# First score pass in the first layer's feed-forward stages: two pairs of tiles at a visit, and visits further apart

## The chip, the cores and the metric

The kernel runs on one core of one Trainium2 chip. TensorE (PE) multiplies matrices, ScalarE (ACT) and VectorE (DVE) work on what it leaves in PSUM, GpSimd (POOL) and SyncE (SP) do small work and issue transfers. The metric is the time of one execution on the device, in microseconds (us). Before the change it is 2257.18 us, the median of 3 runs (2246.01 to 2261.7).

## The reference

Four transformer layers with conditioning work on x of shape (4, 512, 288): 4 batch entries, 512 tokens, 288 channels, 16 heads of 18 channels. Each layer computes six modulation vectors from the conditioning input, then an attention block and a feed-forward block:

```
mod = silu(c) @ w_adaln + b_adaln            # shift, scale, gate, twice
h = ln(x) * (1 + scale) + shift
q, k, v = split(h @ w_qkv + b_qkv)
attn = softmax(q @ k^T * 18**-0.5)           # per head, 512 x 512
x = x + gate * (attn @ v @ w_proj + b_proj)
x = x + gate2 * ffn(ln(x) * (1 + scale2) + shift2)
```

In the first layer the feed-forward block is a mixture of 4 experts, each 288 -> 1152 -> 288. A gate picks the top 2 for each token, but all four are computed for all tokens and weighted. The other layers have one such network. In the third layer the attention is of another kind (each token's 16 heads attend to one another; it has its own steps, with "2" or "b" in their names), and the gelu is the exact one.

## The kernel before, in words

**Steps.** `plan` writes one list of steps, and each of the five engine programs walks this list and issues its own part of every step, with semaphores between them. So the list's order is the order on every engine's queue. What is put next is decided by a planned time, `pe[0]`, which adds up the entries of `PE_NS` (ns of TensorE, 1650 for an `fc1`, 400 for an `fc2`, 230 for an `s1`).

**Stages.** A stage of the main loop has number i, 0 to 16. It holds the attention of image i (an image is one batch entry in one layer: i // 4 is the layer, i % 4 the entry), woven with the norm and the q/k projection of image i + 1; then the v projection of image i + 1; then the feed-forward block of image i - 1, woven with two side streams: `mid(i)` (turning the attention output, projection, residual, norm, routing) and `side`, the first score pass of image i + 1.

**Two score passes.** The softmax needs the maximum of each row of scores. The first pass (`s1`) computes a score tile of one head and one block of 128 queries (54 rows of contraction: 18 channels in three blocks of high and low parts; 512 keys wide), and VectorE reduces it to 128 row maxima (`s1_max`, L1496). The two heads of a pair (x = 0, 1) lie on the upper and the lower half of the partitions. An image has 8 pairs x 4 query blocks x 2 heads = 64 such tiles. After four heads (a group g) `rows` transposes the maxima (L1743), and they are stored as further rows of QS (L1111). The second pass (`s2`, L1750) computes the transposed scores with the maxima subtracted, ScalarE exponentiates them (L1345), and `av` (L1760) multiplies with v. The attention has 16 such steps, `st`; step st needs the rows of group st // 4. Each step also takes one turn of the first pass (`s1_step`): of the same image as long as tiles are left, then of the next image, once its q and k have landed.

**The first pass as a stream.** `s1_steps(i)` is a generator. A turn (one `next`) puts one visit: two `s1` tiles, one for each head of the pair, then their two `s1_max`. A `rows` step takes a turn of its own, DEFER = 1 query block into the next pair. Until the transfers of q and k are due (QK_LAND), turns do nothing. `weave(main, sides)` takes the main stream step by step and, at each of its yields, gives a side stream a turn if its gap of planned time has passed since its last one. For the first layer's feed-forward stages the gap of the first pass is `S1_NS[0]` = 5000 (i = 2 to 4, all four experts) and `S1_0_NS[2]` = 4000 (i = 1, experts 1 to 3).

**The feed-forward main stream.** `ffn_steps` works in units of two hidden tiles of 128 x 256 tokens: an `fc1` (14 matmuls, L1856) into bank 6 or 7, ScalarE's two gelus, VectorE's `hid` (the low part of the hidden tile, L1626), and, two units later (LAG), the four `fc2` (3 matmuls each, L1871, and one with the bias, L1869, at the start of a half) into banks 2 and 3. It yields after each `fc1` and after each pair of `fc2`. At the end of a half the gated result is read out (`res`, L1561). In the second half of each expert, weights of the next ones are split into high and low parts by background steps (ScalarE L1375, VectorE L1394 and L1396).

**Banks.** A score tile fills a whole PSUM bank. `ring()` deals banks out in turn: in a first-layer feed-forward stage RING_B = (0, 1, 4, 5), which the middle steps use as well; in the attention RING_A = (0, 1, 7). The second pass uses banks 4 and 5, and 2 and 3. TensorE waits (`may_fill`) until the last reader of the bank is done.

## Time and profile before

| | |
|---|---|
| median of 3 runs | 2257.18 us |
| the profiled execution, its span | 2257.0 us |
| TensorE busy | 2033.0 us, 90% |
| VectorE busy | 1335.6 us, 59% |
| ScalarE busy | 1143.6 us, 51% |
| row maxima (L1496), all 768 | 490.4 us of VectorE, 682 ns each |
| first-pass score tiles (L1737), all 768 | 226.1 us of TensorE |

The span is that of one execution which the hardware profiler recorded. Busy time is the union of an engine's instructions; matmuls overlap in the records, so their durations may not be added up: the distance from one start to the next tells what one costs. In the trace, the first layer's feed-forward blocks lie about at 193 to 428 us (image 0), 497 to 648 (image 1), 710 to 860 (image 2) and 923 to 1069 (image 3), and the attention behind them at 436 to 493 (image 2), 652 to 707 (image 3), 864 to 920 (image 4) and 1070 to 1132 (image 5). The granted clock of TensorE is 1.00 at 2.4 GHz and 0.50 at 1.2 GHz.

### The profile page before, as it was taken

To read this page: it belongs to the slowest core of one execution; us is meant where nothing else is said; L and a number is where in the kernel's file an instruction comes from. 1 tells how busy PE (TensorE), PEld (TensorE's weight loads), DVE (VectorE), ACT (ScalarE), POOL (GpSimd) and SP (SyncE) were. 2 spreads that over 40 slices of the span, in tenths; PEclk is the share of its full clock that TensorE was granted. 3 is DMA by queue.
4 is the path that set the end of the run, shared out by engine and by line. 5 is a ranking of instruction groups with operands and counts; after the bars stand their busy time and mean duration, and the time that the engine had idled before them with its cause. 6 is when DMAs were issued, how large, how long until landed. Compare 5 with 4: busy or idle time off the path is not lost.

```text
span 2257.0 us, 38969 instructions
## 1 busy us (share of the span) xinstructions
PE 2033.0 (90%) x15592; PEld 1509.0 (67%) x15592; DVE 1335.6 (59%) x2940; ACT 1143.6 (51%) x1705; POOL 207.4 (9%) x311
## 2 busy tenths in 40 slices
PE   6978899899989998999799899899888898999898
PEld 4347388658966994788375657788786556464658
DVE  4757637756774767476556673462444849484833
ACT  2444624574655456445626464552443464637373
POOL 2000001202100211012010000011000000000001
PEclk9787989899989999999889999998898998999999
DMA  5333332343333233333322313346254141314011
GB/s 158 77 123 57 100 95 72 79 111 86 89 77 106 72 89 76 96 94 88 94 72 35 103 17 65 73 88 109 34 95 130 7 121 26 99 11 115 9 14 25
DMA packets 204731, 173.97 MB, mean 77 GB/s; under 512 B 54822, under 2 KB 164678, under 8 KB 204550
## 3 DMA queue, kind: packets, MB, share of 16 engines
q1 hardware_dynamic: 197974, 158.76, 30.1%
q0 software_dynamic: 6576, 12.71, 2.1%
q8 instruction: 124, 2.03, 0.4%
q14 instruction: 57, 0.47, 0.1%
HBM read 125.57 MB, written 40.11 MB: 73 GB/s over the span
## 4 chain that ended last, share of the span: by engine, by line
PE 63%; DVE 18%; ACT 12%; DMA 3%; issue 2%; SPq 2%; POOL 0%; ACTq 0%; POOLq 0%; DVEq 0%
PE PSA L1856 16%; PE PSA L1871 13%; DVE MX L1496 7%; PE PSA L1647 5%; PE PSA L1760 5%; PE PSA L1737 5%; ACT PB L1345 4%; PE PSA L1707 4%; PE PSA L1750 4%; PE PSA L1719 2%; DVE FL L1396 2%; PE PSA L1780 1%; ACT FH L1375 1%; PE PSA L1670 1%; DVE HH L1626 1%
## 5 line engine op out<-in xcount | busy, mean ns | idle before, releaser
L1496 DVE TENSOR_REDUCE MX<-PSA 128x1 f32<-128x512 f32 x768 | 490.4, 682 | 296.9 <-PE PSA L1737 293.2
L1856 PE MATMUL PSA<-A,FH 128*128 128x256 f32 x2520 | 445.3, 292 | 12.5 <-DVE HH L1626 9.6
L1871 PE MATMUL PSA<-FH,HH 128*128 128x288 f32 x2016 | 447.7, 313 | 2.0 <-DVE HH L1626 2.0
L1382 ACT ACTIVATE HH<-PSA 128x512 fp32r<-128x512 f32 x252 | 150.4, 597 | 572.5 <-PE PSA L1856 567.3
L1345 ACT ACTIVATE PB<-PSA 128x1024 f32<-128x1024 f32 x384 | 370.9, 1025 | 102.5 <-PE PSA L1750 101.8
L1856 PEld LDWEIGHTS PSA<-A,FH 128*128 128x128 f32 x2520 | 364.9, 195 | 34.6 <-issue 17.3
L1871 PEld LDWEIGHTS PSA<-FH,HH 128*128 128x128 f32 x2016 | 329.7, 195 | 42.3 <-issue 38.0
L1871 PE MATMUL PSA<-FL,HH 128*128 128x288 f32 x1008 | 303.7, 301 | 0.0
L1737 PE MATMUL PSA<-KS,QS 54*128 54x512 f32 x768 | 226.1, 517 | 40.0 <-DVE MX L1496 14.0
L1255 POOL TENSOR_TENSOR X<-X,TM 128x288 f32<-128x288 f32 x128 | 101.1, 808 | 1496.7 <-DVE TM L1561 1496.6
L1760 PE MATMUL PSA<-PB,VT 128*32 128x512 f32 x1536 | 219.6, 637 | 0.0
L1750 PE MATMUL PSA<-QS,KS 56*128 56x512 f32 x768 | 172.6, 498 | 51.2 <-ACT PB L1345 27.2
L1626 DVE TENSOR_TENSOR HH<-PSA,HH 128x512 fp32r<-128x512 f32 x252 | 171.8, 682 | 76.1 <-ACT PSA L1383 75.8
L1856 PE MATMUL PSA<-A,FL 128*128 128x256 f32 x1008 | 208.0, 288 | 6.3 <-DVE FL L1396 6.3
L1871 PEld LDWEIGHTS PSA<-FL,HH 128*128 128x128 f32 x1008 | 196.8, 195 | 0.0
L1750 PEld LDWEIGHTS PSA<-QS,KS 56*128 56x128 f32 x768 | 70.2, 198 | 165.4 <-ACT PB L1345 84.8
L1737 PEld LDWEIGHTS PSA<-KS,QS 54*128 54x128 f32 x768 | 94.3, 203 | 115.1 <-DVE MX L1496 37.8
L1856 PEld LDWEIGHTS PSA<-A,FL 128*128 128x128 f32 x1008 | 159.3, 195 | 10.3 <-DVE FL L1396 9.1
L1383 ACT ACTIVATE PSA<-PSA 128x512 f32<-128x512 f32 x252 | 149.5, 593 | 0.0
L1375 ACT CAST FH<-ST 128x672 fp32r<-128x672 f32 x171 | 123.2, 748 | 32.9 <-PE PSA L1871 13.5
L1396 DVE TENSOR_TENSOR FL<-ST,FH 128x544 fp32r<-128x544 f32 x171 | 125.3, 733 | 5.3
L1707 PE MATMUL PSA<-A,WQ 128*126 128x512 f32 (+1 forms) x300 | 95.5, 421 | 23.0 <-DVE HH L1490 9.5
(166 smaller groups left out, 2261.5 us busy)
## 6 DMA issues: line engine op xcount, KB each, us to landing
qkd<-HH SPq DMA_DIRECT2D x48, 504.0 KB
ST<-in_L_cond_w SPq DMA_DIRECT2D x51, 432.0 KB
ST<-in_L_cond_w SPq DMA_DIRECT2D x102, 192.0 KB
QS<-qkd SPq DMA_DIRECT2D x88, 144.0 KB
KS<-qkd SPq DMA_DIRECT2D x88, 144.0 KB
QS<-qkd SPq DMA_DIRECT2D x144, 72.0 KB
KS<-qkd SPq DMA_DIRECT2D x144, 72.0 KB
ST<-in_L_cond_w SPq DMA_DIRECT2D x153, 48.0 KB
```

The costliest lines, as they stand in the source:

```text
L1345: e.activation(pbf[st % 3][:, p * 1024:(p + 1) * 1024], PSA[:, bk * 512:(bk + 2) * 512], ACT.Exp, scale=SCALE).then_inc(free[bk], 1)
L1382: e.activation(r(HH[u][:, 0, :]), PS[bk][:, :], gelu)
L1383: e.activation(PS[bk][:, :], PS[bk][:, :], gelu).then_inc(s_gelu, 1)
L1396: e.tensor_tensor(r(lo), ST[k % 2][:, s0:s0 + nl], hi[:, 0:nl], ALU.subtract).then_inc(s_wlo, 1)
L1496: e.reduce_max(MX[p // 2 % 2][:, col:col + 1], PS[bk][:, :], axis=AX.X).then_inc(free[bk], 1)
L1626: e.tensor_tensor(r(HH[u][:, 1, :]), PS[bk][:, :], HH[u][:, 0, :], ALU.subtract).then_inc(free[bk], 1)
L1707: m = e.matmul(PS[bk][0:M, :], r(w_), r(x_), start=(z == 0), stop=(z == 6))
L1737: e.matmul(PS[bk][:, :], r(QS[64 * x:64 * x + 54, p, q * 128:(q + 1) * 128]), r(KS[64 * x:64 * x + 54, p, :]), start=True, stop=True).then ...
L1750: m = e.matmul(PS[bk + x][:, :], r(KS[64 * x:64 * x + 56, 2 * g + p, kt * 128:(kt + 1) * 128]), r(QS[64 * x:64 * x + 56, 2 * g + p, :]), s ...
L1760: m = e.matmul(PS[bk][32 * hh:32 * hh + 32, :], VT[:, kt, h * V1:h * V1 + 32], PB[st % 3][:, hh, :], start=(kt == 0), stop=(kt == 3))
L1856: m = e.matmul(PS[bk][:, s_ * 256:(s_ + 1) * 256], r(w_), r(x_[:, half * 256:(half + 1) * 256]), start=(z == 0), stop=(z == 6))
L1871: m = e.matmul(PS[bk][:, 0:C], r(HH[u][:, c, tk]), r(w_), start=False, stop=(j == NCH - 1 and z == 2))
```

## The change

In the feed-forward stages of the first layer (i = 1 to 4) a turn of the first pass puts two query blocks: four `s1` tiles in four banks, then their four maxima, where the block is even; an odd one, left over from a visit of the attention, is done alone first. The gap grows to 8000 ns for all of them. In the attention and in the later layers a visit stays at two tiles. `S1_NS[0]` also stands in the weave behind the feed-forward block.

```
-S1_0_NS = (0, 2500, 4000)
-S1_NS = (5000, 400, 3000)
+S1_0_NS = (0, 2500, 8000)
+S1_NS = (8000, 400, 3000)
...
-    hurry, stream = [False], []
+    hurry, stream, two_visits = [False], [], [False]
...
-            for q in range(QT):
+            q = 0
+            while q < QT:
                 while not hurry[0] and pe[0] < qk_at.get((i, min(g, 2)), 1e9) + QK_LAND:
                     yield
-                bks = []
-                for x in range(2):
-                    bk = ring()
-                    put("s1", i, p, q, x, bk, qk_n[min(g, 2)])
-                    bks.append(bk)
-                for x in range(2):
-                    put("s1_max", p, q, x, bks[x])
+                visit = range(q, q + (2 if two_visits[0] and q % 2 == 0 else 1))
+                q = visit[-1] + 1
+                bks = {}
+                for qq in visit:
+                    for x in range(2):
+                        bk = ring()
+                        put("s1", i, p, qq, x, bk, qk_n[min(g, 2)])
+                        bks[qq, x] = bk
+                for qq, x in bks:
+                    put("s1_max", p, qq, x, bks[qq, x])
                 yield
-                if late is not None and q == DEFER:
+                if late is not None and DEFER in visit:
                     rows(*late)
                     late = None
                     yield
...
+        two_visits[0] = bool(i) and kind == 0
         if i:
             weave(ffn_steps(i - 1, (1, 2, 3) if i == 1 else None), ((m, MID_NS[kind], MID_AT[i == 11] if L == 2 else 0),
                                        (side, S1_0_NS[2] if i == 1 else S1_NS[kind], 0)))
         weave(m, ((side, S1_NS[kind], 0),))
+        two_visits[0] = False
```

## Rows read from the trace of the kernel before

**Rows 1.** The page: span, and busy time of TensorE.

```profile
span 2257.0 us, 38969 instructions
PE 2033.0 (90%) x15592; PEld 1509.0 (67%) x15592; DVE 1335.6 (59%) x2940; ACT 1143.6 (51%) x1705; POOL 207.4 (9%) x311
```

**Rows 2.** Windows: length, busy us of each engine (instructions), granted clock, DMA share.

```profile
497.00:648.00 151.00, 147.05 (x1075) 136.64 (x1073) 101.18 (x207) 77.84 (x130) 22.58 (x34) 0.98 0.30 85
652.00:707.00 55.00, 49.40 (x284) 20.60 (x285) 32.74 (x79) 38.14 (x46) 0.12 (x1) 0.91 0.49 116
```

**Rows 3.** Windows for the maxima alone: PE (transposes), PEld, then DVE.

```profile
497.00:648.00 151.00, 0.55 (x2) 0.18 (x2) 24.45 (x38) 0.98 0.30 85
923.00:1069.00 146.00, 0.54 (x2) 0.18 (x2) 23.25 (x37) 1.00 0.30 78
652.00:707.00 55.00, 0.66 (x2) 0.17 (x2) 15.49 (x25) 0.91 0.49 116
1070.00:1132.00 62.00, 0.56 (x2) 0.18 (x2) 16.93 (x27) 0.89 0.37 100
```

**Rows 4.** Timeline of TensorE, feed-forward: start, duration, line, tiles, count.

```profile
560.68 0.28 PE L1856 MATMUL PSA<-A,FH 98*128 98x256 f32 x1
560.80 0.30 PE L1869 MATMUL PSA<-B,ON 128*128 128x288 f32 x1
...
563.40 0.28 PE L1856 MATMUL PSA<-A,FH 98*128 98x256 f32 x1
563.61 0.49 PE L1737 MATMUL PSA<-KS,QS 54*128 54x512 f32 x2
564.03 0.54 PE L1871 MATMUL PSA<-FH,HH 128*128 128x288 f32 x2
```

**Rows 5.** Timeline of TensorE in image 0's attention: three tiles in a row.

```profile
91.44 0.62 PE L1737 MATMUL PSA<-KS,QS 54*128 54x512 f32 x3
```

**Rows 6.** Timeline of image 2's attention: steps with and without a visit.

```profile
463.30 0.73 PE L1750 MATMUL PSA<-QS,KS 56*128 56x512 f32 x4
463.87 0.39 PE L1737 MATMUL PSA<-KS,QS 54*128 54x512 f32 x2
...
466.24 1.19 PE L1707 MATMUL PSA<-A,WQ 128*126 128x512 f32 x4 [0.98 <-DVE HH L1490]
...
468.04 0.73 PE L1750 MATMUL PSA<-QS,KS 56*128 56x512 f32 x4
...
471.53 0.73 PE L1750 MATMUL PSA<-QS,KS 56*128 56x512 f32 x4
...
464.30 1.29 DVE L1496 TENSOR_REDUCE MX<-PSA 128x1 f32<-128x512 f32 x2 [0.83 <-PE PSA L1737]
465.50 0.68 DVE L1490 TENSOR_TENSOR HH<-PSA,HH 126x512 fp32r<-126x512 f32 x1
```

**Rows 7.** Timeline: hidden tile's low part, and the fc1 two units later.

```profile
501.21 0.69 DVE L1626 TENSOR_TENSOR HH<-PSA,HH 128x512 fp32r<-128x512 f32 x1 [0.30 <-ACT PSA L1383]
502.05 0.36 PE L1856 MATMUL PSA<-A,FH 128*128 128x256 f32 x1 [0.62 <-DVE HH L1626]
...
567.49 0.69 DVE L1626 TENSOR_TENSOR HH<-PSA,HH 128x512 fp32r<-128x512 f32 x1
569.03 0.64 PE L1856 MATMUL PSA<-A,FH 128*128 128x256 f32 x4
...
634.83 0.68 DVE L1626 TENSOR_TENSOR HH<-PSA,HH 128x512 fp32r<-128x512 f32 x1
636.85 0.52 PE L1856 MATMUL PSA<-A,FH 128*128 128x256 f32 x3
```

**Rows 8.** Timeline and a window at the seam to image 3's attention.

```profile
650.84 1.28 DVE L1496 TENSOR_REDUCE MX<-PSA 128x1 f32<-128x512 f32 x2
652.26 1.22 PE L1750 MATMUL PSA<-QS,KS 56*128 56x512 f32 x4 [3.83 <-DVE MX L1496]
...
652.00:661.00 9.00, 7.95 (x29) 2.95 (x33) 7.30 (x20) 5.80 (x7) 0.12 (x1) 0.50 0.88 167
```

## The prediction

> **What bounds the kernel now.** The page first: one profiled execution of 2257.0 us, TensorE busy for 90% of it [rows 1]. Then the windows of the stages that the edit touches. In a feed-forward window of the first layer (497 to 648 us) TensorE is busy for 147.05 of 151 us and VectorE for 101.18; in the attention window behind it (652 to 707 us) TensorE for 49.40 of 55 us [rows 2]. So a feed-forward stage ends with TensorE's own work, and there I may only gain by giving TensorE less to do; an attention stage has idle time to gain. Then the same windows for the row maxima alone, one of which follows each first-pass score tile: 38 and 37 in two feed-forward windows, 25 and 27 in two attention windows, 0.64 us of VectorE each (24.45 / 38) [rows 3]. Last the timelines: what a visit costs TensorE among the feed-forward matmuls [rows 4], what more tiles in a row cost [rows 5], what a visit costs in an attention step [rows 6], how close VectorE's part of the hidden tile comes to the next fc1 [rows 7], and the seam of the two stages [rows 8].
>
> **How many visits there will be.** PE_NS gives the planner's clock. 36 units of one fc1 (1.65) and four fc2 (1.6) are 117 us, the middle steps some 10, the score tiles the rest. The loop yields after an fc1 and after each fc2 pair, so a gap is rounded up to the next yield. Before, a gap of 5 becomes mostly 6.5 (two units) plus the visit's own 0.46: about 21 turns, of which 2 go to the row transposes: 19 visits, 38 tiles, as counted [rows 3]. After, a gap of 8 becomes 8.1 (two and a half units) plus 0.92: about 15 turns, 3 for transposes, 12 double visits: 48 tiles. An image has 64 tiles (8 pairs, 4 row blocks, 2 heads), and the step list has 8 of them in the attention before, behind the landing of its keys. For images 3, 4 and 5 that leaves 64 - 8 - 48 = 8 tiles to their own attention instead of 18. For image 2 (the stage with i = 1, 27 units, old gap 4, rounded to about 4.3 for one visit and now 8.1 for a double one) the counts stay level, 36 or so against 38.
>
> **Term A, TensorE in the feed-forward stages.** From the last fc1 matmul to the first fc2 matmul it is 0.12 us (560.68 to 560.80), with a visit between 0.63 us (563.40 to 564.03): a visit adds 0.52 us (between 0.63 and 0.66 less 0.12) [rows 4]. The two tiles of a pair of heads run side by side; a third tile starts 0.23 us behind them, since three take 0.62 us where two take 0.39 [rows 5, 6]. So a double visit adds 0.52 + 0.23 = 0.75 us, and not 1.04: what is saved is one entry and one exit, 0.29 us. Images 3 to 5: 19 x 0.52 = 9.9 against 12 x 0.75 = 9.0, three times -0.9 = -2.7. Image 2: 9.9 against 9 x 0.75 = 6.8, and one visit more is left to the attention: -3.1. A = -5.8. The other bound: were the 0.29 us a cost of each pair, A would be 3 x (12 x 1.04 - 9.9) + (9 x 1.04 - 9.9) = +7.2. I take -5.8, because the row of three tiles shows the third without it. The Trainium skill (TensorE Tiling (Array Packing), Key Properties) says that a change of the tiling mode drains TensorE; by it the price belongs to the change between 54-row and full-height matmuls, and the sum would be -5.8 rather than +7.2. The trace's third tile agrees.
>
> **Term B, the attention of images 3 to 5.** Two steps of the same make stand side by side: with a visit and a qk tile, 463.30 to 468.04, 4.74 us; with the qk tile alone, 468.04 to 471.53, 3.49 us [rows 6]. The difference, 1.25 us, is mostly a wait of 0.98 us: ring banks 0, 1 and 7 are filled by two score tiles and one qk tile, so each qk tile needs the bank of the one before it, whose subtraction (HH, 465.50) stands behind two maxima (464.30, 1.29 us) on VectorE. Images 3, 4 and 5 each have three such steps, the seventh to the ninth; with 8 tiles left the visits end in the fourth. Two of the three are as in the row: -2.5 us. The first qk step also waits for the turned activations, so it gives 0 to 1.25: I take 0.6. Two steps with a transpose lose a visit worth about 0.25 us: -0.5. Together -3.6 each (bounds -2.5 and -4.5), times three: -10.8. Image 2's one visit more falls on a qk step: +1.2. B = -9.6 (bounds -6.3 and -12.5).
>
> **Term C, what four maxima in a row delay.** They hold VectorE for 2.6 us where two hold it for 1.3. Queued behind them in program order are the hidden tile's low part (L1626), the weight splits and the gated residuals; fc1 two units later waits for the first through its bank, fc1's low terms for the second, fc2 at the start of a half for the third. The slack of that fc1 behind its hidden tile, where a visit stands ahead of it (16 times in the window), was 0.15 us at the first (501.90 to 502.05), 0.85 at 569.03, and 1.34 at the last (635.51 to 636.85) [rows 7]; the 16 lie between 0.15 and 7.0. A double visit delays VectorE by 1.28 more and TensorE itself by 0.23, so slack under 1.05 turns into a stall. Spread over the 16 that is 0.12 us a visit, for twelve visits 1.4. For splits and residuals I add about 1 us a stage, the size of the small waits that these windows have already (4 us idle in 151, [rows 2]). Three stages with 2.4, the shorter one 1.8: C = +9. Bounds: nothing, and twice as much, +18.
>
> **Term D, the seam.** At the end of image 1's feed-forward the last visit's maxima (650.84, 1.28 us) hold a bank that the second score pass needs; TensorE idles for 3.83 us [rows 8]. Four maxima hold it for up to 1.3 us more, if the last visit is again that late; if it comes a gap earlier, 1.3 us are won. Bounds -1.2 and +1.3 in each of three seams; by the yields a visit falls at the end again, so I take +0.5 each: D = +1.5.
>
> Costing nothing: the extra two banks of a visit. Ring B has four, the visit takes all, and the next middle step (at least 0.8 us of fc2 later) needs the first of them, whose maximum has started by then; ScalarE's and the DMA queues' work is neither added nor passed, only the row stores (L1111) come a few us earlier, with their group of heads long before its use. The gap of 8 also holds in the weave that empties the middle steps behind a stage with i = 0, where visits stay single; of these steps none or a few are left by then.
>
> **Sum:** -5.8 - 9.6 + 9 + 1.5 = -4.9, so 2257.0 - 4.9 = 2252 us. The median before, 2257.18, is the profiled time within 0.2 us, so it needs no shift.
>
> **The rivals.**
> 1. *VectorE's backlog wins (slower).* Place: the feed-forward stages, behind each of some 45 double visits. If the 1.05 us is never absorbed, C is 45 x 1.05 = 47 and the time 2257 - 15.4 + 47 + 1.5 = 2290. For it: slacks of 0.15 and 0.85 us, VectorE at 67%, and more where weights are split. Against: slack of over 1.3 us in most units. It decides the sign at C = 14 us (0.3 us a visit), and passes 1% at about 0.8 us a visit.
> 2. *The cover holds.* C and D nothing, A and B as worked out: 2257 - 15.4 = 2242; with the best bounds of B and D, 2235.
> 3. *Attention gives nothing back.* If the qk steps wait for the turned activations or for ScalarE's copies as long as they now wait for HH, B is +1.2 and the time 2257 - 5.8 + 1.2 + 10.5 = 2263. Against: the qk step without a visit, which waited for neither.
> 4. *The clock.* Right behind the idle seam, from 652 to 661 us, the granted clock is 0.50, that is 1.2 GHz, after 3.83 us in which TensorE did nothing [rows 8]. A longer seam could lengthen such a stretch: matmuls there take twice as long, so 3 us more of it in three seams cost some 5 us: 2257. The Trainium skill (TensorE: Matmul & The Clock Gate, Why this matters for your kernels) warns of idle gaps between bursts, which speaks against a late double visit; the trace's seam agrees.
> 5. *The change hardly does what it says*: if visits meet fewer yields than I count and 40 tiles are made, A is near -4, B near -2, C near 7, D as before: 2257 + 2.5 = 2260.
>
> **How the numbers follow.** Forecast as worked out (net gain under 1%): 0.50; the cover holds 0.18; backlog 0.15, about half of it over 1%; no gain in attention 0.08; clock 0.05; few visits 0.04. Range: A + B at their best with C and D at nothing or better reach 2235; C doubled, B's weak end and longer seams reach 2257 - 5.8 - 6.3 + 18 + 3.9 = 2267, with a little clock 2269; A's other bound, +7.2, would carry that to 2280 and is left out, since a row speaks against it. That leaves out most of the backlog's high end and the extreme of the low one: 2236 to 2269. One per cent, about what a measurement of this kernel can tell, is 22.6 us: faster than 2234.6 has 0.07 (the good ends of rival 2), slower than 2279.8 has 0.07 (rival 1), the rest 0.86.
>
> **What would show each step.** A: score visits of four tiles among fc1 and fc2, with about 0.87 us from the matmul before to the one behind. Count: 48 or so maxima in the feed-forward windows of images 1 to 3. B: in images 3 to 5 qk steps of 3.5 us and no wait for HH there; attention windows shorter by 3 to 4 us. C: waits of fc1 for L1626 and L1396, of fc2 for TM, growing from about 2 to about 4 us a stage. D: the idle time before the first second-pass matmul at 3 to 5 us. I am wrong if the waits of C sum to over 15 us, if the attention windows keep their length, or if the seams move by more than 2 us each.

## The result: 1.25% slower, and the profile after

The changed kernel takes 2285.06 us, the median of 4 runs (2279.86 to 2289.14), against 2259.44 us (2246.01 to 2262.4, 4 runs) for the kernel before in the same comparison: a ratio of 1.0125, 95% interval 1.0092 to 1.0159. I had forecast 2252 us, and 2236 to 2269 as the range. The time lies above the range, and the sign is wrong: of the outcomes I named, it is the third, slower by over 1%, to which I had given 0.07.

Line numbers of the kernel after are six higher: L1743 is `s1`, L1502 `s1_max`, L1862 `fc1`, L1877 `fc2`, L1756 `s2`, L1713 `qk`. The page of its profiled execution, span and busy time, answers to [rows 1]:

```profile
span 2283.7 us, 38968 instructions
PE 2043.3 (89%) x15592; PEld 1514.3 (66%) x15592; DVE 1338.2 (59%) x2940; ACT 1143.2 (50%) x1705; POOL 209.0 (9%) x311
```

The span is 26.7 us longer than before. TensorE issues the same 15592 matmuls, yet is busy for 10.3 us more, and idle for 16.4 us more. VectorE and ScalarE have the work that they had. Of the 10.3 us, 7.5 lie ahead of 289.8 us (230.1 us busy before, 237.5 after), where TensorE has the same matmuls in the same order in both and the granted clock is 0.85 before and 0.81 after: that part isn't the change's. What the change costs has to be read from the stages that it touches.

To find the place I cut both traces at the same points: a stage from the start of the v projection of image i to the first second-pass matmul of image i (it holds a feed-forward block and the seam), and the attention from there to the next v projection. First the kernel before, its four stages and four attentions (windows: stretch, length, busy us of PE, PEld, DVE, ACT, POOL with their instructions, granted clock, DMA share, GB/s):

```profile
286.90:436.30 149.40, 140.91 (x952) 126.60 (x950) 86.77 (x177) 60.75 (x103) 21.25 (x32) 0.92 0.30 81
493.10:652.30 159.20, 151.42 (x1106) 140.73 (x1104) 106.07 (x218) 80.18 (x135) 24.12 (x36) 0.98 0.31 88
706.60:863.70 157.10, 149.85 (x1105) 139.34 (x1103) 102.82 (x213) 77.41 (x132) 24.34 (x37) 0.99 0.29 76
919.60:1070.30 150.70, 145.24 (x1077) 134.53 (x1075) 100.00 (x196) 75.17 (x129) 20.22 (x32) 1.00 0.31 82
436.30:493.10 56.80, 48.31 (x280) 19.88 (x280) 34.60 (x91) 39.22 (x48) 7.88 (x11) 0.88 0.36 91
652.30:706.60 54.30, 48.96 (x282) 20.13 (x282) 32.34 (x76) 37.84 (x46) 0.00 (x0) 0.91 0.49 117
863.70:919.60 55.90, 48.74 (x280) 20.12 (x281) 34.61 (x79) 39.03 (x48) 1.87 (x3) 0.91 0.44 108
1070.30:1131.70 61.40, 48.88 (x283) 19.74 (x284) 34.05 (x77) 40.49 (x48) 4.27 (x7) 0.89 0.37 100
```

And the kernel after, the same eight stretches; the last row is a window of the maxima and row transposes alone (PE, PEld, DVE), which answers to [rows 3]:

```profile
289.80:447.30 157.50, 142.16 (x951) 128.17 (x949) 85.61 (x174) 60.71 (x103) 22.60 (x34) 0.90 0.28 77
506.60:678.70 172.10, 156.16 (x1119) 143.92 (x1117) 115.31 (x230) 80.09 (x135) 24.89 (x36) 0.95 0.30 85
729.80:895.10 165.30, 152.09 (x1118) 141.35 (x1116) 110.07 (x226) 77.17 (x132) 26.88 (x39) 0.98 0.27 73
946.50:1103.80 157.30, 148.65 (x1083) 138.00 (x1081) 104.47 (x204) 75.12 (x129) 19.76 (x30) 0.98 0.29 77
447.30:506.60 59.30, 48.65 (x283) 20.08 (x283) 36.55 (x94) 39.22 (x48) 6.27 (x10) 0.89 0.33 82
678.70:729.80 51.10, 47.42 (x265) 18.67 (x266) 24.08 (x62) 37.88 (x46) 0.00 (x0) 0.90 0.48 115
895.10:946.50 51.40, 47.60 (x271) 19.23 (x271) 27.18 (x66) 39.03 (x48) 0.00 (x0) 0.91 0.45 116
1103.80:1158.10 54.30, 45.95 (x276) 18.68 (x275) 30.09 (x69) 40.37 (x48) 5.10 (x8) 0.94 0.41 111
...
506.60:678.70 172.10, 0.82 (x3) 0.27 (x3) 31.78 (x52) 0.95 0.30 85
```

The attentions fell from 228.4 to 216.1 us, by 12.3: the gain came. The four stages grew from 616.4 to 652.2, by 35.8. Length less TensorE's busy time gives its idle time: 29.0 us before, 53.1 after, so 24 us of the 36 are idle time, more than twice the 10.5 that I had allowed in terms C and D. The granted clock fell in each of the four; twice the length times one less the clock is the time at 1.2 GHz, 35 us before and 62 us after where it is summed from the clock's own record. Half of such time is lost, so that is about 13.5 us in this pair of executions. It is firm only in part. In the stages of images 3 to 5 it is 12 us at 1.2 GHz before and 31 after, and runs with the same matmuls in the same order repeat it (10.5 in experiment 8, 28 in experiment 11): a loss of some 10 us. In image 2's stage it is 24 and 31 us; but with that stage's matmuls as before, full maxima and single visits, seven other runs have 11 to 30 us there, and a stage of 144.5 to 152.6 us. So the 3.6 us of the clock there can be chance, and the 8 us by which that stage grew can be off by some us either way. With the visits' -5.8 us (below) and some 4 us that I can't place, this is the whole of it.

### The profile page after: what moved, and what is told of

It reads as the page before. It is cut to its first block, busy times and chain, and to the rows that moved or that the text cites. A ratio compares the mean times of both kernels' runs of the same rounds, so it can differ in the third digit from the quotient of the medians.

```text
span 2283.7 us, 38968 instructions
## 1 busy us (share of the span) xinstructions
PE 2043.3 (89%) x15592; PEld 1514.3 (66%) x15592; DVE 1338.2 (59%) x2940; ACT 1143.2 (50%) x1705; POOL 209.0 (9%) x311
## 4 chain that ended last, share of the span: by engine, by line
PE 63%; DVE 18%; ACT 13%; issue 2%; DMA 2%; SPq 1%; POOL 0%; ACTq 0%; POOLq 0%; DVEq 0%
PE PSA L1862 15%; PE PSA L1877 12%; DVE MX L1502 7%; PE PSA L1766 6%; PE PSA L1653 5%; PE PSA L1743 4%; PE PSA L1756 4%; PE PSA L1713 4%; ACT PB L1351 4%; DVE FL L1402 2%; PE PSA L1676 2%; PE PSA L1725 2%; ACT FH L1381 1%; PE PSA L1786 1%; ACT HH L1388 1%
## 5 line engine op out<-in xcount | busy, mean ns | idle before, releaser
L1502 DVE TENSOR_REDUCE MX<-PSA 128x1 f32<-128x512 f32 x768 | 485.7, 681 | 206.4 <-PE PSA L1743 202.7
L1862 PE MATMUL PSA<-A,FH 128*128 128x256 f32 x2520 | 450.7, 295 | 16.7 <-DVE HH L1632 9.0
L1877 PE MATMUL PSA<-FH,HH 128*128 128x288 f32 x2016 | 442.4, 310 | 2.7 <-DVE HH L1632 2.7
L1862 PEld LDWEIGHTS PSA<-A,FH 128*128 128x128 f32 x2520 | 370.0, 198 | 40.1 <-issue 15.5
L1877 PEld LDWEIGHTS PSA<-FH,HH 128*128 128x128 f32 x2016 | 327.7, 194 | 38.6 <-issue 33.1
L1877 PE MATMUL PSA<-FL,HH 128*128 128x288 f32 x1008 | 301.7, 299 | 0.0
L1743 PE MATMUL PSA<-KS,QS 54*128 54x512 f32 x768 | 222.6, 509 | 53.1 <-DVE A L1478 14.3
L1766 PE MATMUL PSA<-PB,VT 128*32 128x512 f32 x1536 | 224.9, 651 | 0.0
L1862 PE MATMUL PSA<-A,FL 128*128 128x256 f32 x1008 | 211.5, 292 | 15.0 <-DVE FL L1402 14.8
L1756 PE MATMUL PSA<-QS,KS 56*128 56x512 f32 x768 | 174.4, 506 | 53.4 <-ACT PB L1351 29.3
L1632 DVE TENSOR_TENSOR HH<-PSA,HH 128x512 fp32r<-128x512 f32 x252 | 171.5, 681 | 84.9 <-ACT PSA L1389 84.6
L1877 PEld LDWEIGHTS PSA<-FL,HH 128*128 128x128 f32 x1008 | 194.8, 193 | 0.0
L1756 PEld LDWEIGHTS PSA<-QS,KS 56*128 56x128 f32 x768 | 70.9, 201 | 170.5 <-ACT PB L1351 84.7
L1743 PEld LDWEIGHTS PSA<-KS,QS 54*128 54x128 f32 x768 | 94.3, 204 | 129.9 <-DVE MX L1502 37.5
L1862 PEld LDWEIGHTS PSA<-A,FL 128*128 128x128 f32 x1008 | 161.5, 197 | 21.2 <-DVE FL L1402 20.7
L1381 ACT CAST FH<-ST 128x672 fp32r<-128x672 f32 x171 | 122.4, 747 | 26.7 <-PE PSA L1877 14.4
L1713 PE MATMUL PSA<-A,WQ 128*126 128x512 f32 (+1 forms) x300 | 94.9, 418 | 17.3 <-DVE A L1472 10.2
```

The source lines that it names most:

```text
L1502: e.reduce_max(MX[p // 2 % 2][:, col:col + 1], PS[bk][:, :], axis=AX.X).then_inc(free[bk], 1)
L1632: e.tensor_tensor(r(HH[u][:, 1, :]), PS[bk][:, :], HH[u][:, 0, :], ALU.subtract).then_inc(free[bk], 1)
L1713: m = e.matmul(PS[bk][0:M, :], r(w_), r(x_), start=(z == 0), stop=(z == 6))
L1743: e.matmul(PS[bk][:, :], r(QS[64 * x:64 * x + 54, p, q * 128:(q + 1) * 128]), r(KS[64 * x:64 * x + 54, p, :]), start=True, stop=True).then ...
L1756: m = e.matmul(PS[bk + x][:, :], r(KS[64 * x:64 * x + 56, 2 * g + p, kt * 128:(kt + 1) * 128]), r(QS[64 * x:64 * x + 56, 2 * g + p, :]), s ...
L1766: m = e.matmul(PS[bk][32 * hh:32 * hh + 32, :], VT[:, kt, h * V1:h * V1 + 32], PB[st % 3][:, hh, :], start=(kt == 0), stop=(kt == 3))
```

## Where the idle time and the low clock come from

Rows of what TensorE waited for over the four stages and the three attentions between them (engine and line, the releaser, us in total, times, longest), before (287 to 1070 us):

```profile
PE PSA L1856 <- DVE FL L1396: 6.3, 12, 1.8
...
PE PSA L1707 <- DVE HH L1490: 5.7, 7, 1.0
```

and after (289 to 1104 us):

```profile
PE PSA L1862 <- DVE FL L1402: 14.8, 19, 3.7
PE PSA L1756 <- DVE MX L1502: 9.8, 2, 5.0
...
PE PSA L1743 <- DVE A L1487: 5.3, 2, 2.7
PE PSA L1743 <- DVE A L1490: 5.2, 4, 1.3
PE PSA L1743 <- DVE A L1478: 5.1, 4, 1.3
```

Three of these are score tiles (L1743) that wait for the low part of a *turned chunk* of activations (L1478, L1487, L1490). Such a wait hardly existed before. A score tile reads nothing of these chunks: what it shares with them is the ring of banks. Per kernel, over the four stages, TensorE waited 17.4 us ahead of score tiles, 1.2 us before; ahead of `fc1` 23.7 us, 11.2 before; at the seams 9.8 us, 9.5 before.

One of the two longest such waits, at its place in the timeline (start, duration, engine, line, tiles, count, idle time before it with its releaser; weight loads and transfers are left out):

```profile
512.04 0.60 PE L1699 MATMUL PSA<-ID,OT 128*128 128x128 f32 x4
512.28 1.28 ACT L1388 ACT_TABLE_LOAD   x1 [1.33 <-PE PSA L1862]
512.57 0.73 PE L1743 MATMUL PSA<-KS,QS 54*128 54x512 f32 x3
513.57 0.60 ACT L1388 ACTIVATE HH<-PSA 128x512 fp32r<-128x512 f32 x1
514.07 0.59 ACT L1389 ACTIVATE PSA<-PSA 128x512 f32<-128x512 f32 x1
514.58 0.59 ACT L1317 CAST A<-PSA 128x512 fp32r<-128x512 f32 x1
...
515.20 0.69 DVE L1487 TENSOR_TENSOR A<-PSA,A 128x512 fp32r<-128x512 f32 x1 [7.62 <-ACT A L1317]
515.81 2.47 DVE L1502 TENSOR_REDUCE MX<-PSA 128x1 f32<-128x512 f32 x4
515.95 0.79 PE L1743 MATMUL PSA<-KS,QS 54*128 54x512 f32 x1 [2.65 <-DVE A L1487]
```

And the windows right behind it, columns as above:

```profile
516.00:522.00 6.00, 6.00 (x26) 5.56 (x27) 5.47 (x8) 1.78 (x3) 0.00 (x0) 0.50 0.49 134
522.00:531.00 9.00, 7.69 (x56) 6.75 (x56) 4.53 (x9) 4.64 (x8) 0.00 (x0) 1.00 0.65 175
```

At 512.04 four transposes fill a ring bank; the double visit is put right behind them. Three of its tiles start at once, at 512.57. The fourth needs the bank of the transposes, since the visit takes all four. That bank is free only when ScalarE has copied it, behind a table load of 1.28 us and two activations, and VectorE has subtracted. So the fourth tile starts at 515.95, after 2.65 us in which TensorE did nothing, and everything else in its queue stands behind it. In the windows the clock is 0.50, that is 1.2 GHz, for the window of 6 us behind it, in which TensorE is busy throughout, and 1.00 after that. In experiment 11, where this stage has the same matmuls in the same order, the same wait (2.66 us, until 496.70) is followed by a shorter such stretch, 0.50 from 498.0 to 501.4 us and 1.00 from there to 507. In the kernel before the visit behind the same transposes (499.09 us) takes two banks that lie clear of the one just dealt, and waits for nothing. The Trainium skill (TensorE: Matmul & The Clock Gate, Why this matters for your kernels) advises against idle gaps between bursts of matmuls. The trace agrees, with these 2.65 us and the 0.50 behind them, and shows it for a gap shorter than those that the page names.

The `fc1` waits, at one place, same columns:

```profile
817.47 0.73 PE L1743 MATMUL PSA<-KS,QS 54*128 54x512 f32 x4
818.01 2.48 DVE L1502 TENSOR_REDUCE MX<-PSA 128x1 f32<-128x512 f32 x4 [2.05 <-PE PSA L1743]
...
820.84 0.73 DVE L1402 TENSOR_TENSOR FL<-ST,FH 128x544 fp32r<-128x544 f32 x1
...
821.62 0.51 PE L1862 MATMUL PSA<-A,FL 128*128 128x256 f32 x2 [2.65 <-DVE FL L1402]
```

Four maxima hold VectorE until 820.49, a weight's low part follows (to 821.57), and `fc1`'s low terms need it: the delay that the prediction's term C named.

## Experiments

All comparisons are with the kernel before, run on the same chip. "Ring waits" below are TensorE's idle time ahead of score tiles, "fc1 waits" that ahead of `fc1`, "half clock" the time at 1.2 GHz, each summed over the four stages of the profiled execution. That is one execution of each kernel, not its median one; and ahead of image 2's stage, where TensorE's matmuls and their order are the same in all of them, these executions take from 280.6 to 295.9 us. So a few us of half clock, or of a profiled span, tell nothing between two runs.

**1. Many single visits.** The kernel before, with one constant changed, so that about the tiles of the changed kernel move into the stages, two at a visit.

```
-S1_NS = (5000, 400, 3000)
+S1_NS = (4000, 400, 3000)
```

> The kernel before with one number changed: S1_NS[0] from 5000 to 4000, so that single visits (two tiles) come at about the tile rate of the changed kernel (54 tiles in the stages of images 3 to 5, where the changed kernel has 46 to 52 and the one before 38 to 40). Theory R (the bank ring: a double visit fills all four ring banks and waits for a turned chunk): no such wait here, attention of images 3 to 5 shorter by 3 to 7 us each as in the changed kernel, the feed-forward stages longer only by some 7 visits of 0.52 us each, so 2257 - 14 + 11 = 2254 (2246 to 2262). Theory L (it is the higher rate of tiles in the feed-forward stage that delays VectorE and the weight splits, whatever the size of a visit): feed-forward stages 7 to 12 us longer each, 2275 or more.

2267.05 us, ratio 1.0044 (1.002 to 1.0067). It lies between what the two theories said: ring waits 2.5 us and half clock 31 us, as the kernel before has them, but fc1 waits 23.2 us. The tiles themselves also moved (54, 54 and 52 maxima in the stages of images 3 to 5, which take 169.9, 166.9 and 159.9 us). The attention of image 4 reads:

```profile
876.50:928.30 51.80, 48.14 (x267) 19.00 (x267) 24.72 (x62) 38.46 (x47) 0.00 (x0) 0.89 0.47 118
```

It is as short as in the changed kernel (51.40). So moving the tiles costs what it gains and some 10 us more even with single visits (202 maxima in the four stages, where the changed kernel has 188 and the one before 160); the double visits, with image 2's new gap, lose a further 18 us on top.

**2. The gaps alone.** The kernel before with single visits and both gaps at 8000.

```
-S1_0_NS = (0, 2500, 4000)
-S1_NS = (5000, 400, 3000)
+S1_0_NS = (0, 2500, 8000)
+S1_NS = (8000, 400, 3000)
```

> The kernel before with the two gaps of 8000 and single visits: 22 to 28 tiles in the feed-forward stages, 28 to 34 left to the attention. The price of a tile in the attention against one in the feed-forward stage: feed-forward stages shorter by 5 visits of 0.52 us plus what waits they made (3 to 4 us each), attention longer by about 1.3 us for each qk step that gets a visit and 0.3 for the others (3 to 5 us each). Theory R: 2257 to 2265. Theory L: the feed-forward stages gain more than that (5 to 8 us each), 2240 to 2250.

2352.0 us, 1.0436 (1.0393 to 1.0479), slower than either theory said. The stages are shorter, 600.0 us in sum, but the attentions take 91.6, 74.8, 76.9 and 81.8 us. What TensorE waits for in the first of them:

```profile
PE PSA L1750 <- DMA QS<-M: 15.6, 3, 7.5
```

With 28 to 34 tiles left to each attention, the second pass waits for the stores of the row maxima, which both theories had left out. That is a limit to placing fewer tiles in the stages.

**3. Double visits at the old gaps.** The kernel after, with `S1_0_NS[2]` = 4000 and `S1_NS[0]` = 5000.

```
-S1_0_NS = (0, 2500, 8000)
-S1_NS = (8000, 400, 3000)
+S1_0_NS = (0, 2500, 4000)
+S1_NS = (5000, 400, 3000)
```

> The changed kernel with the old gaps (5000 and 4000): double visits only, 56 to 58 tiles in the stages of images 2 to 5, none left to their attention. Theory R: about as many or more visits meet a turned chunk (11 turned or projected banks a stage), so the feed-forward stages lose what the changed kernel loses and a little more, attention gains 2 to 4 us more each: 2278 to 2292. Theory B (four maxima in a row delay the hidden tile's low part and the splits): more visits, more delay: 2290 to 2305.

2269.85 us, 1.0067 (1.0035 to 1.0098), less than either theory said. Ring waits 7.4 us, half clock 46 us, fc1 waits 20.6 us; the seam's idle time is nearly gone (0.3 us for 9.8), since the tiles run out before it. The profiled execution is the slowest of the six (2282.22 us). More frequent double visits lose less than rare ones; the ring waits follow where the visits fall, and not how many there are (0.65 us in each of the stages of images 4 and 5, which hold 58 tiles).

**4. Double visits kept clear of a bank just dealt.** The kernel after; `weave` puts a side stream's turn off while a ring bank has been dealt in the last 3000 ns of planned time.

```
         ring_n[0] += 1
+        dealt[0] = pe[0]
...
-                if pe[0] >= last[n]:
+                if pe[0] >= last[n] and not (n and two_visits[0] and pe[0] - dealt[0] < 3000):
```

> The changed kernel, where a double visit is put off to a later yield while a ring bank was dealt less than 3000 planned ns ago (turned chunk, projection): the same counts of tiles in the stages of images 3 to 5 (52, 50, 46), 36 instead of 40 for image 2. Theory R: the waits of a fourth tile for a turned chunk go (7.0 + 5.2 + 2.6 + 2.6 = 17 us in the trace of the changed kernel), and some of the half-clock stretches behind them: 2285 - 17 - 5 = 2263 (2255 to 2270). Theory B or L: the waits of fc1 for the splits stay and the time is 2275 or more.

2295.53 us, 1.0179 (1.0143 to 1.0215): slower still, and no verdict on the ring. The edit took only 4.5 us of the ring waits away (12.9 left), put visits off so far that image 2 has 36 tiles in its stage and an attention of 73.0 us with 11.0 us of waits for the row stores, and fc1 waits rose to 35.3 us.

**5. A near visit split in two.** The kernel after; where a bank was dealt in the last 3000 ns, a double visit is put as two single ones, the second at the next yield.

```
+                near = pe[0] - dealt[0] < 3000
+                two = two_visits[0] and q % 2 == 0
+                owed[0] = two and near
-                visit = range(q, q + (2 if two_visits[0] and q % 2 == 0 else 1))
+                visit = range(q, q + (2 if two and not near else 1))
...
-                if pe[0] >= last[n]:
+                if n and owed[0]:
+                    owed[0] = False
+                    next(side, None)
+                elif pe[0] >= last[n]:
```

> The changed kernel, where a visit that finds a ring bank dealt less than 3000 planned ns ago takes two tiles and leaves the other two to the very next yield: the same counts of tiles in each stage as in the changed kernel, and no shift of the later visits. Theory R: the waits of the fourth tile for a turned chunk (7.0, 5.2, 2.6 and 2.6 us in the four stages of the changed kernel's trace) go, and the half-clock stretches behind the longest of them: 2285 - 17 - 3 = 2265 (2260 to 2272), with the gain in image 2's and image 3's stages. Theory B (maxima in a row delay the weight splits, which fc1 then waits for): those fc1 waits stay at 5 us a stage, and the time falls by less than 8 us.

2287.25 us, 1.0127 (1.0096 to 1.0158), no gain. The ring waits were not removed (18.1 us), they moved. TensorE's waits of score tiles in its stages (289 to 1110 us):

```profile
PE PSA L1750 <- DVE A L1485: 5.1, 4, 1.3
PE PSA L1750 <- DVE TM L1574: 4.9, 3, 1.7
```

The second half of a visit, a yield later, now meets the banks that the projection fills (TM). Both attempts share a fault: they look at the bank just dealt, not at whether the visit wants it before its reader is through.

**6 and 7. Short maxima in both kernels.** In the stages i = 1 to 4 `s1_max` reads 64 of the 512 keys; the number of instructions, the banks and the order stay. First in the kernel after, then in the kernel before.

```
...
-                    e.reduce_max(MX[p // 2 % 2][:, col:col + 1], PS[bk][:, :], axis=AX.X).then_inc(free[bk], 1)
+                    e.reduce_max(MX[p // 2 % 2][:, col:col + 1], PS[bk][:, 0:64 if light else T], axis=AX.X).then_inc(free[bk], 1)
```

> The changed kernel, with the row maxima of the first layer's feed-forward stages (i = 1 to 4) taken over 64 of the 512 keys (part of the computation is left out): a burst of four holds VectorE for about 0.7 us instead of 2.5. Theory B: the waits of fc1 for split weights and hidden parts shrink to what they are with few maxima, 1 to 2 us a stage, and the seam to 2 us; with the ring waits still there but shorter: 2285 - 4 x 5 = 2265. Against the kernel before with the same short maxima the loss shrinks from 26 us to under 12. Theory R: the fourth tile's wait ends with the turned chunk, not with maxima: 2275 to 2282, and the loss against its twin stays at 20 or more.

> The kernel before with the same short maxima in the same stages (part of the computation is left out), the twin of the run above. Its feed-forward windows wait little for VectorE, so 2 to 4 us a stage at the seams and for splits: 2245 to 2253 on theory B and on theory R alike.

2271.19 us, 1.0062 (1.0035 to 1.0089), and 2244.08 us, 0.9935 (0.9912 to 0.9957). Each gains 14 to 15 us, and they stay 27 us apart, where the full kernels are 26 apart; theory R had said 20 or more, theory B under 12. The stage of image 3 in the one after, then in the one before:

```profile
505.60:671.40 165.80, 153.59 (x1118) 142.72 (x1116) 93.31 (x231) 79.00 (x133) 25.36 (x36) 0.97 0.30 85
```

```profile
487.20:640.90 153.70, 149.55 (x1105) 139.25 (x1103) 87.89 (x217) 79.05 (x133) 23.36 (x35) 0.99 0.32 90
```

VectorE is busy for 56 to 57% of both, yet the one stage is 12.1 us longer, and 8.1 us of that is idle time. Of the waits, the ring's remain (16.5 us against 1.5), and fc1's grow by half as much as in the full kernels (17.6 against 11.1). So the time that four maxima take is not what makes the change slower on balance; it is half of the growth of the fc1 waits, about 6 us.

**8. Low parts ahead of the maxima.** The kernel before; in the attention the pending low parts are settled before a turn of the first pass. It tries the wait of [rows 6] by itself.

```
+            for what in list(rest):
+                settle(what)
             for _ in range(2 if i == 0 else 1):
                 s1_step()
```

> The kernel before, where in each attention step the pending low parts of turned chunks and qk tiles (VectorE) are put ahead of the first pass's turn and its maxima. Theory B of the prediction (a qk tile waits 0.98 us for the subtraction that stands behind two maxima): that wait goes in every attention step that has both, some 2 to 3 steps in each of 12 images, 0.98 us each: 2257 - 25 to 30 = 2230 (2225 to 2240). Rival: the wait passes to the first pass's tiles, whose maxima are now later, and half the gain is lost: 2243 to 2250.

2262.4 us, 1.0002 (0.998 to 1.0024): neither the 2230 us that I expected nor the rival's 2243 to 2250. The wait for HH is gone (7.6 us in nine places before, over the same attentions), and a qk step takes 3.70 us with a visit (starts 468.75 and 472.45 us) and 3.47 without (472.45 and 475.92), near what I had worked out from [rows 6]; but the gain went into other waits of the same attentions. The timeline first:

```profile
468.75 0.73 PE L1752 MATMUL PSA<-QS,KS 56*128 56x512 f32 x4
469.32 0.40 PE L1739 MATMUL PSA<-KS,QS 54*128 54x512 f32 x2
...
472.45 0.73 PE L1752 MATMUL PSA<-QS,KS 56*128 56x512 f32 x4
```

Its waits of TensorE over the attentions of images 2 to 5 (436 to 1138 us):

```profile
PE PSA L1752 <- DMA QS<-M: 9.4, 4, 3.6
```

Before, it was 2.3 us in two places. A wait taken out of an attention that still holds 14 to 18 tiles is for the most part given back at the row stores; it counts in the changed kernel only because the tiles leave as well.

**9. Single visits near the middle steps.** The kernel after, but while `mid` turns chunks and projects, a turn is a single visit with a gap of 4000; elsewhere double at 8000. The stages hold as many tiles as in the changed kernel (42 single and 26 double visits, 188 tiles, where it has 2 and 46).

```
-                visit = range(q, q + (2 if two_visits[0] and q % 2 == 0 else 1))
+                visit = range(q, q + (2 if two_visits[0] and not busy[0] and q % 2 == 0 else 1))
...
-                    last[n] = pe[0] + gap
+                    last[n] = pe[0] + (4000 if n and two_visits[0] and busy[0] else gap)
...
+        busy[0] = True
         yield from turn_o((i + 1) % 2)
...
+        busy[0] = False
         yield from norm(i)
         for _ in range(W_MID):
             yield
+        busy[0] = True
         yield from turn_x(norm_of[i], (i + 1) % 2, L, 2, b)
+        busy[0] = False
```

> The changed kernel, with single visits at a gap of 4000 while the middle steps use the ring for turned chunks and projections, and double visits at 8000 otherwise; the counts of tiles in every stage are those of the changed kernel. The account of the stages so far: their length is a fixed part plus 0.52 or 0.75 us a visit, plus TensorE's idle time, plus half of the time at half clock. Theory R (ring): the 17 us in which score tiles wait for a turned chunk fall to about 2, some of the half-clock time (62 us in the changed kernel against 35) goes with them, the single visits cost 3 more: 2285 - 15 - 6 + 3 = 2267 (2260 to 2273). Theory P (any other placing of visits than that before makes fc1 wait for VectorE, the waits only change their name): 2278 or more.

2272.53 us, 1.0048 (1.0026 to 1.007), 12.5 us under the changed kernel. By its ratio it is still 11 us above the kernel before, where the changed kernel is 28 us above it (by the medians 16 and 26). Ring waits 3.3 us for 17.4, half clock 40 us for 62, fc1 waits unchanged at 24.0. The stage of image 3:

```profile
495.40:661.40 166.00, 151.91 (x1119) 140.03 (x1117) 114.15 (x230) 80.73 (x136) 24.94 (x36) 0.98 0.31 87
```

The waits, from 286 to 1084 us:

```profile
PE PSA L1747 <- DVE MX L1506: 2.7, 3, 1.1
PE PSA L1747 <- DVE A L1485: 1.9, 1, 1.9
```

Against the changed kernel's row of this stage: busy time 156.16 down to 151.91 with the same 1119 matmuls, and the clock up from 0.95 to 0.98. Only the width and the spacing of the visits near the middle steps differ. The four stages fell by 17.8 us (652.1 to 634.3): ring waits -14.1, other small waits +3.5, clock -11 (half of 22), more visits +5.8 (42 x 0.52 + 26 x 0.75 for 46 x 0.75 + 2 x 0.52), and -2 not placed. So the ring's waits and the low clock with them were real losses of the change. They are about half of its loss, from 0.4 of it by the medians to 0.6 by the ratios. (Of the 22 us at 1.2 GHz, 17 fell in the stages of images 3 to 5; the 5 in image 2's stage are within its spread.)

**10. Visits only behind fc1.** The kernel after, with turns of the first pass allowed only at the yield behind an `fc1`. In the changed kernel the fc1 waits right behind a visit were 9.5 us in 19 places, 1.7 us in 22 before.

```
-                if pe[0] >= last[n]:
+                if pe[0] >= last[n] and not (n and two_visits[0] and not behind_fc1[0]):
```

> The changed kernel, with turns of the first pass only at the yield right behind an fc1 (mostly 9.75 planned us apart): 36, 44, 46 and 42 tiles in the four stages instead of 40, 52, 50 and 46. Theory P: the waits of fc1 came with visits right ahead of an fc1 (0.6 us each there, 0.1 behind one): they fall from 24 to 12 us; fewer visits -2; but the attention gets 20 tiles back, +6; one visit still meets a turned chunk in three stages. 2285 - 12 - 2 + 6 - 6 = 2271. If the place of a visit does not matter: 2284 to 2290.

2278.15 us, 1.0075 (1.0048 to 1.0101). The fc1 waits were to fall to 12 us; they rose to 29.0, none of it right behind a visit: the place of a visit between `fc1` and `fc2` is not their cause. Image 2's attention again grew (73.1 us), since its stage makes only 36 tiles and leaves more to it.

**11 and 12. Image 2's stage undone, and the old gap with it.** In the stage i = 1 single visits at 4000 again, everything else as after; then also the gap of 5000 in the other stages.

```
-        two_visits[0] = bool(i) and kind == 0
+        two_visits[0] = i > 1 and kind == 0
-S1_0_NS = (0, 2500, 8000)
+S1_0_NS = (0, 2500, 4000)
```

```
-S1_NS = (8000, 400, 3000)
+S1_NS = (5000, 400, 3000)
```

> The changed kernel, with the stage i = 1 (first pass of image 2) as before: single visits, gap 4000. In the traces that stage and the attention behind it are 10.5 us longer in the changed kernel than before, nothing of it bought back: 2285 - 10.5 = 2275 (2270 to 2279). If the loss is general (clock, or carried from stage to stage): 2280 or more.

> Double visits at the old gap of 5000 for images 3 to 5 (56 to 58 tiles, none left to the attention), the stage i = 1 as before. By the traces of the run with double visits at old gaps, its loss stood in the stage of image 2 (215 against 206 us), and images 3 to 5 were within 1.5 us of before: 2270 - 9 = 2261 (2255 to 2265), level with the kernel before. If the stage i = 1 costs as much without doubles there: 2268 or more.

2271.52 us, 1.0051 (1.003 to 1.0072), and 2269.65 us, 1.004 (1.0013 to 1.0067). About half of the loss goes with the double visits of a stage in which I had counted on level tiles and a gain of 3 us (7.0 of the 17.4 us of ring waits were there). This half and that of experiment 9 overlap, as experiment 13 shows. The old gap on top gives nothing that can be told (2261 us was expected): image 3's stage there is still 171.5 us, with 6.5 us of ring waits and 20 us of half clock.

**13 to 15. Repairs together.** The edits of experiment 9 and the first diff below; then the second as well; then the third as well.

```
-S1_0_NS = (0, 2500, 8000)
+S1_0_NS = (0, 2500, 4000)
...
-        two_visits[0] = bool(i) and kind == 0
+        two_visits[0] = i > 1 and kind == 0
```

```
-S1_NS = (8000, 400, 3000)
+S1_NS = (5000, 400, 3000)
```

```
-                    last[n] = pe[0] + (4000 if n and two_visits[0] and busy[0] else gap)
+                    last[n] = pe[0] + (5000 if n and two_visits[0] and busy[0] else gap)
```

> The changed kernel with both repairs: the stage of image 2 as before, and single visits (gap 4000) near the turned chunks in the stages of images 3 to 5. If the ring waits with their half-clock time and the stage of image 2 carry the loss and do not overlap beyond image 2's own ring waits: 2272.5 less what image 2's stage still lost there (2.7 us): 2269 (2264 to 2272), where 5 us of waits of fc1 remain that the attention's gain has to pay. If the account by stage is complete, images 3 to 5 are at +3.6, +3.5 and -1.9 us against before: 2262.

> As the run with both repairs, but with the old gap of 5000 between double visits: 56 to 58 tiles, nothing left to the attention of images 3 to 5. The seam then has no late maxima ahead of it (0 against 5 us in the traces at this gap), the fc1 waits are 4 to 5 us a stage. By the account: images 3 to 5 each level with before or 1 to 2 us under it: 2255 (2250 to 2261), the best of the double visits. If the attention without its own tiles gives nothing more than one with four: 2262 or more.

> As the run above with a gap of 5000 instead of 4000 for the single visits near the turned chunks; more visits then stand right behind an fc1 (9 to 10 a stage) and fewer right ahead of one (3 instead of 5). If the place ahead of an fc1 costs: 2 to 4 us under the run above, 2252. If not, level with it.

2269.58 us, 1.0067 (1.0043 to 1.0091); 2267.66 us, 1.0047 (1.0029 to 1.0065), where 2255 was expected; 2262.33 us, 1.0017 (0.9999 to 1.0034). The first shows that the two repairs don't add up: ring waits are 2.3 us and half clock 36 us, and fc1 waits still 23.2. In the second the seams are gone (0.3 us) and half clock is 22 us (10 in the stages of images 3 to 5, where the kernel before has 12), but the fc1 waits stay (22 us), and in the attentions of images 2 to 4 TensorE waits 14.4 us for ScalarE's exponentials (`s2` for the tiles PB), for 8.4 in the changed kernel.

The third is the best kernel with double visits, level with the kernel before at best. Its profiled execution, 2250.21 us, is the fastest of its twelve. No run here that does the whole computation is faster than the kernel before.

## Why the prediction was wrong, step by step

**The step that failed: "Costing nothing: the extra two banks of a visit".** I asked whether the middle step *behind* a visit finds a free bank, and it does. I did not ask whether the visit itself does, when it takes all four banks and a middle step stands *ahead* of it. The readers of that step's bank are ScalarE and VectorE, with whatever is queued on them, and here that took over 2 us more. Measured: 16 us more of ring waits (1.2 to 17.4), where I had nothing. Experiment 9 shows it by itself: the same tiles at narrower visits near the middle steps, ring waits 3.3 us, 12.5 us faster.

That is about half of the loss. Experiment 9 is still 11 to 16 us slower than the kernel before, and experiment 1 some 10 us, without one double visit more than there was. So a second step failed with it: that the tiles come into the feed-forward stages for the price of their visits and a few us of delay (term C). In experiment 9 the stages' idle time is 42.5 us for 29.0 before, and 12.8 of these 13.5 us are fc1 waits, against attentions that are 10 us shorter; its visits cost what they did before (41 us), so term A's gain is gone as well.

**The clock, rival 4.** I had it only at the seams, and put 5 us and a chance of 0.05 on it. Time at 1.2 GHz rose by 27 us in this pair, a loss of 13.5 us, of which some 10 (the stages of images 3 to 5) repeat in other runs. Much of that follows the ring waits: in these three stages it was 31 us, and 15 in experiment 9, where they were nearly gone. It isn't tied to them alone: the changed kernel's clock also falls to 0.50 behind a wait of 2.65 us ahead of `fc1` (until 821.62 us), and experiment 13 has few ring waits and 24 us of it in these stages, experiment 14 as few and 10.

**Term A was right.** The double visit answers to [rows 4]:

```profile
571.45 0.28 PE L1862 MATMUL PSA<-A,FH 98*128 98x256 f32 x1
571.66 0.73 PE L1743 MATMUL PSA<-KS,QS 54*128 54x512 f32 x4
572.32 0.53 PE L1877 MATMUL PSA<-FH,HH 128*128 128x288 f32 x2
```

From 571.45 to 572.32 it is 0.87 us, so the visit adds 0.75 over the 0.12 of [rows 4], as worked out, where two single visits add 1.04. The counts were a little off (76 single visits and 45 double ones in the forecast), and the sum came out the same: before there were 78 single visits and one place where two followed one another, after 46 double and 2 single ones: 46 x 0.75 + 2 x 0.52 - 78 x 0.52 - 0.75 = -5.8 us. The rule of the Trainium skill (TensorEngine Tiling (Array Packing), Key Properties), that changing the tiling mode drains the engine, agrees with that: one entry and one exit, 0.29 us, are saved for each double visit.

**The counts were near.** Before there were 42, 40, 40 and 38 tiles in the stages of images 2 to 5; the windows of [rows 3] are shorter than the stages, so the 38 and 37 read from them are too few, and the forecast's 21 turns don't come out of its own figures (some 136 us of planned time by 6.96 are 20). After there were 40, 52, 50 and 46 tiles, forecast 36 and three times 48; to the attentions went 16, 4, 8 and 12, forecast 8 for the last three.

**Term B was right in its mechanism and in its sum.** The steps of image 3's attention, where the visits have ended, answer to [rows 6]:

```profile
702.12 0.73 PE L1756 MATMUL PSA<-QS,KS 56*128 56x512 f32 x4
...
705.60 0.74 PE L1756 MATMUL PSA<-QS,KS 56*128 56x512 f32 x4
```

A qk step of 3.48 us, and behind it one of 3.46 (to 709.06), with no wait for HH, for 4.7 before. The attentions changed by +2.5, -3.2, -4.5 and -7.1 us, in sum -12.3; forecast +1.2 and three times -3.6, -9.6, the best bound -12.5. Image 5's -7.1 lies outside the bound of 4.5 that I gave each, and no run tells why. So rival 3 (attention gives nothing) fell. Experiment 8 adds what the term did not see: the wait for HH is worth something only when the tiles leave with it.

**Term C was in the bounds, above its value.** fc1 waits rose by 12.5 us (11.2 to 23.7), forecast +9 with the rest of C in it, bound 18. I had called myself wrong if the waits of C sum to over 15 us: 23.7 is over that, the growth is not. The 0.12 us a visit also doesn't come out of the two short slacks that the prediction shows, which give 0.07 (0.90 and 0.20 us over 16). The growth alone would not have turned the sign: I had put that at 14 us. Rival 1, the backlog, is thus there in its place but not at its price: experiments 6 and 7 give it some 6 us, and take it out as the cause of the loss. The other half of the fc1 waits' growth stays open. It came with single visits (experiment 1, 23.2 us), with fewer of them (experiment 2, 20.6), and in every placing of double ones (18.3 to 35.3), so neither the burst nor the place between `fc1` and `fc2` explains it; that any shift of the visits against the weight splits breaks a fit which the kernel before happens to have is a guess that no run here tests.

**Term D.** At the seam to image 3's attention the wait answers to [rows 8] and grew by 1.1 us:

```profile
678.68 1.22 PE L1756 MATMUL PSA<-QS,KS 56*128 56x512 f32 x4 [4.96 <-DVE MX L1502]
```

The next seam grew by 1.0 us, the last fell by 1.6 us, its 1.56 us gone, which is past the bound of 1.2. Over all seams it is +0.3 us, forecast +1.5.

**The sum in their place**, of the profiled executions: stages -5.8 (visits) + 16.2 (ring) + 12.5 (fc1) + 0.3 (seams) - 5 (other small waits) + 13.5 (clock) + 4 (not placed) = +36; attentions -12.3; the rest of the program +3.3, most of it ahead of image 2's v projection, which starts at 289.8 for 286.9 us, with the same matmuls ahead of it, so by chance. That is +27, and the spans are 26.7 apart. Without the ring waits and the clock this sum would be -3, close to the -4.9 that I forecast. But that is arithmetic within one pair of traces, and no run reached it: where experiment 9 took the ring waits away, it paid 5.8 us more for its visits and stayed 11 to 16 us above the kernel before. The term I dismissed in a sentence carries about half of the loss; that the rest nearly adds up to the forecast is partly luck, since C's growth above its value is met by 5 us fewer of other small waits and by an attention gain above its value.

## What to carry to other kernels

Where two streams share banks dealt in turn, a wider burst of one must be asked two questions: whether what follows it finds a bank, and whether the burst itself does, given what stands ahead of it and whose queue releases that; a burst that takes the whole ring waits for the slowest reader of any bank in it. An engine that is 95% busy over its stages (587 of 616 us) loses such a wait in full, and may lose as much again to its clock behind it (2.65 us of waiting, then over 6 us at 0.50). Saving set-up of an instruction (here 0.29 us a visit) is worth little beside one wait of 2.65 us, and work moved out of one stage should be priced in the other by the waits that it brings, as experiment 1 shows with no wider burst at all.

## What the runs showed of the hardware that I had not expected

- A single wait of 2.65 us of TensorE in a stage in which it is otherwise busy was followed by a window of 6 us at 0.50, and the clock was back at 1.00 behind it; in experiment 11 the same wait was followed by one of 3.4 us. Over four stages of 652 us 62 us ran at 1.2 GHz, 35 of 616 before.
- The time of a stretch moves by several us from run to run with nothing changed in it: the first 1159 matmuls, the same in all 17 traces here, took 280.6 to 295.9 us, and 82 to 116 us of that were at 1.2 GHz.
- Busy time is not work: with the same matmuls TensorE was busy for 10.3 us more (7.5 of them ahead of any change, at a clock of 0.81 for 0.85), and in one stage 4.3 us less (156.16 to 151.91) when the ring waits went.
- The copy that frees a bank on ScalarE stood behind a load of an activation table at the gelu's line, 1.28 us; that is over a third of the chain to the free bank (512.28 to 515.89 us, with two activations, copy and subtraction), and the code of the steps shows nothing of it.
